# Row statistics by one VectorE instruction, and another order of score products, in a two-layer attention tower

## The reference

```
h = token_table[x] * (x != 0) + position_table[...]       # a scan over steps gives the positions
h = h + attention0(layernorm(h))                          # softmax(q k^T / 8) times the normalised rows
h = h + routed_ffn(layernorm(h))                          # relu, two layers of 128, an expert chosen per group of rows
h = h + attention1(layernorm(h))                          # with biases, values and an output projection
h = h + mixture_ffn(layernorm(h))                         # top 2 of 8 gates, gelu, two products for each expert

layernorm(x) = (x - mean(x)) / sqrt(var(x) + 1e-5)        # over the 64 features of a row
```

## Time and profile before

| | |
|---|---|
| runs shown | 999.9, 999.84, 1001.16 us; median 999.9 us |
| profiled execution | 1000.58 us, span of the core 998.8 us |
| TensorE matmuls busy | 933.3 us (93%) |
| VectorE busy | 663.6 us (66%) |
| ScalarE busy | 541.9 us (54%) |
| GpSimd busy | 489.4 us (49%) |
| mean granted clock of TensorE | 0.993 of full speed |
| chain that ended last | TensorE 75%, VectorE 11%, GpSimd 7%, issue 5% |

### The profile page before, as it was taken

One profiled execution on the slowest core, in us unless ns is written; L12 is line 12 of the kernel. 1 busy time (PEld: TensorE's weight loads), 2 busy tenths in 40 slices (PEclk: granted clock), 3 DMA queues, 4 the chain that ended last, 5 costly groups with the idle time before them and its releaser, 6 DMA issues.

```text
span 998.8 us, 21041 instructions
## 1 busy us (share of the span) xinstructions
PE 933.3 (93%) x6247; PEld 635.2 (64%) x6262; DVE 663.6 (66%) x1839; ACT 541.9 (54%) x1067; POOL 489.4 (49%) x779
## 2 busy tenths in 40 slices
PE   4879999999998888889999999998999999999998
PEld 3656666666665555555666666666766667767665
DVE  5868788888887888877888878886434344344331
ACT  1335555555555555544555555555566556655664
POOL 0064545545457888883455554544343433434410
PEclk9989999999999999998999999999999999999999
DMA  3000000000001222210000000000000000000000
GB/s 97 3 1 1 1 0 0 0 0 0 1 1 49 58 63 54 64 33 1 1 1 0 0 0 0 1 1 2 11 17 11 16 16 11 16 15 11 16 11 22
DMA packets 18991, 15.10 MB, mean 15 GB/s; under 512 B 5762, under 2 KB 18946, under 8 KB 18946
## 3 DMA queue, kind: packets, MB, share of 16 engines
q1 hardware_dynamic: 18946, 14.52, 5.2%
HBM read 10.32 MB, written 4.19 MB: 15 GB/s over the span
## 4 chain that ended last, share of the span: by engine, by line
PE 75%; DVE 11%; POOL 7%; issue 5%; DMA 1%; DVEq 0%; ACT 0%; POOLq 0%; SPq 0%
PE bank L1205 12%; PE bank L1027 7%; PE bank L1036 7%; PE bank L1185 7%; PE bank L1028 6%; DVE nmax L723 6%; PE bank L1186 6%; PE bank L1002 6%; PE bank L949 5%; PE bank L1015 4%; PE bank L974 3%; POOL stat L353 2%; PE bank L991 2%; PE bank L1195 2%; PE bank L992 2%
## 5 line engine op out<-in xcount | busy, mean ns | idle before, releaser
L360 POOL TENSOR_TENSOR XN<-XC,stat 128x252 f32<-128x252 f32 x128 | 85.3, 666 | 216.0 <-PE bank L1036 210.9
L723 DVE TENSOR_REDUCE nmax<-bank 128x1 fp32r<-128x512 f32 x256 | 165.0, 686 | 34.6 <-PE bank L1002 29.9
L353 POOL TENSOR_TENSOR stat<-stat,half 128x4 f32<-128x4 f32 x128 | 134.1, 1048 | 91.1 <-DVE stat L641 88.3
L496 ACT ACTIVATE PT<-bank 128x512 f32<-128x512 f32 x256 | 139.5, 595 | 45.9 <-PE bank L1028 45.3
L1036 PE MATMUL bank<-PT,XN 128*64 128x256 f32 x1024 | 138.3, 392 | 0.0
L545 ACT ACTIVATE PT<-bank 128x512 f32<-128x512 f32 x256 | 132.0, 605 | 11.2 <-PE bank L1186 11.1
L468 ACT ACTIVATE OT<-bank 128x256 f32<-128x256 f32 x96 | 36.8, 384 | 183.1 <-PE bank L1036 132.2
L1205 PE MATMUL bank<-PT,W 128*64 128x256 f32 x1024 | 122.8, 382 | 0.0
L446 ACT ACTIVATE X<-bank 128x512 fp32r<-128x512 f32 x128 | 76.3, 596 | 78.7 <-PE bank L949 78.7
L1027 PE MATMUL bank<-QH,X 128*128 128x512 f32 x256 | 116.0, 453 | 0.5 <-ACT Q L489 0.4
L1185 PE MATMUL bank<-X,WH 128*128 128x512 f32 x256 | 107.5, 420 | 0.8 <-ACT K L536 0.8
(11 more groups left out here) (135 smaller groups left out, 1679.7 us busy)
## 6 DMA issues: line engine op xcount, KB each, us to landing
WR<-experts SPq DMA_DIRECT2D x64, 129.0 KB, 2.0
out<-H SPq DMA_DIRECT2D x32, 128.0 KB, 1.7
W<-pack SPq DMA_DIRECT2D x5, 252.5 KB, 4.0
W<-pack SPq DMA_DIRECT2D x1, 251.0 KB, 5.1
W<-pack SPq DMA_DIRECT2D x1, 243.0 KB, 5.7
tk<-tokens SPq DMA_DIRECT2D x1, 64.0 KB, 4.4
route_sb<-route SPq DMA_DIRECT2D x1, 0.2 KB
```

The costliest lines, as they stand in the source:

```text
L353: pl.tensor_tensor(stat[:, par, 3, :], stat[:, par, 2, :], half[:, :], ALU.pow).then_inc(sigma_done, 1)
L496: sc_.activation(PT[:, par, kt, :], bank[4 + kt % 2][:, :], ACT.Exp, scale=SCALE).then_inc(s.e_ready, 1)
L723: v.tensor_reduce(nmax[:, par, t:t + 1], bank[2 + t % 2][:, :], axis=AX, op=ALU.max, negate=True).then_inc(s.max_ready, 1)
```

## The change

The mean and the variance of a row are taken by VectorE's mean-and-variance instruction straight from `H`: one `bn_stats` for each of the four row tiles (64 elements each, six numbers out), and one `bn_aggr` for each, which makes mean and variance of the six. A memset puts epsilon into a small tile and one addition adds the variance to it. The sum, the squares, their sum and the scaling on VectorE go, and so does GpSimd's multiplication by -1/64. GpSimd does one piece of work for each sequence (`norm`): power, subtraction of the mean, and the scaling as before. `XC` has one buffer in place of two.

In the bodies the two halves of VectorE's part have new places. `moments` (the four `bn_stats`) stands, for sequence i+4, in attention after `finish` and ahead of the last two maxima, in the routed stage and in the mixture where the sum was. `moments_end` (the rest) stands after the last maximum, and where the squares were.

In attention, the first two maxima stand ahead of `finish`. On TensorE the products for maxima stand one each after the second and the third score tile and two after the fourth, and the values of all four tiles follow in one row.

The core of the diff (declarations of tiles and semaphores, and the arguments of the calls, are left out):

```diff
-            def norm_centre(s, before, phase, i, par):
-                pool.wait_ge(s.sum_ready, i + 1)
-                pl.tensor_tensor(stat[:, par, 1, :], stat[:, par, 0, :], ninv[:, :], ALU.mult).then_inc(mean_done, 1)
...
-                pl.tensor_tensor(XC[:, par, :, :], hb(i), over(stat[:, par, 1, :], D), ALU.add)\
-                    .then_inc(s.xc_ready, 1)
-
-            def norm_scale(s, before, phase, i, par, lane):
+            def norm(s, before, phase, i, par, lane):
 
                 pool.wait_ge(s.var_ready, i + 1)
-                pl.tensor_tensor(stat[:, par, 3, :], stat[:, par, 2, :], half[:, :], ALU.pow).then_inc(sigma_done, 1)
+                pl.tensor_tensor(rstd[:, :], VE[:, par, :], half[:, :], ALU.pow).then_inc(sigma_done, 1)
+                pl.tensor_tensor(XC[:, :, 1:D], H[:, bass.ds(i, 1), :, 1:D].rearrange("p a t d -> p (a t) d"),
+                                 over(MV[:, par, :, 0], D - 1), ALU.subtract).then_inc(s.xc_ready, 1)
                 pool.wait_ge(sigma_done, phase * NSEQ + i + 1)
+                pool.wait_ge(s.xc_ready, i + 1)
...
-            def norm_sum(s, i, par):
-                v.tensor_reduce(stat[:, par, 0, :], hb(i), axis=AX, op=ALU.add).then_inc(s.sum_ready, 1)
-
-            def norm_squares(s, i, par):
...
+            def moments(s, i, par):
+
+                for t in range(NT):
+                    ins = v.bn_stats(ST[:, par, t, :], H[:, bass.ds(i, 1), t, :].rearrange("p a d -> p (a d)"))
+                ins.then_inc(s.stats_ready, 1)
+
+            def moments_end(s, before, i, par):
+                dve.wait_ge(s.stats_ready, i + 1)
+                if not known(i) or i >= 2:
+                    dve.wait_ge(s.xc_ready, i - 1)
+                elif before is not None:
+                    dve.wait_ge(before.xc_ready, NSEQ - 1 + i)
+                v.memset(VE[:, par, :], EPS)
+                for t in range(NT):
+                    ins = v.bn_aggr(MV[:, par, t, :], ST[:, par, t, :])
+                ins.then_inc(s.pair_ready, 1)
+                dve.wait_ge(s.pair_ready, i + 1)
+                v.tensor_tensor(VE[:, par, :], VE[:, par, :], MV[:, par, :, 1], ALU.add).then_inc(s.var_ready, 1)
 
             def first_norms(s, i):
 
-                par = i % 2
                 dve.wait_ge(h0_ready, i + 1)
-                norm_sum(s, i, par)
-                if i >= 1:
-                    norm_squares(s, i - 1, 1 - par)
-                if i == 3:
-                    norm_sum(s, 4, 0)
-                    norm_squares(s, 3, 1)
+                moments(s, i, i % 2)
+                moments_end(s, None, i, i % 2)
...
                 def body(i, par):
-                    squares_on(s, after, i + 4, par)
-                    sum_on(s, after, i + 5, 1 - par)
                     if has(i + 1):
                         low_parts(i + 1, 1 - par)
+                        maxima(i + 1, 1 - par, range(2))
                     if not known(i) or i >= 1:
                         finish(i - 1, 1 - par)
+                    moments_on(s, after, i + 4, par)
                     if has(i + 1):
-                        maxima(i + 1, 1 - par)
+                        maxima(i + 1, 1 - par, range(2, NT))
+                    moments_end_on(s, before, after, i + 4, par)
...
                     scores(i, par, 1)
+                    if has(i + 1):
+                        scores_for_max(i + 1, 1 - par, 0)
                     if not known(i) or i >= 1:
                         turn_back(s, before, i - 1, 1 - par)
                     scores(i, par, 2)
+                    if has(i + 1):
+                        scores_for_max(i + 1, 1 - par, 1)
                     scores(i, par, 3)
                     if has(i + 1):
-                        scores_for_max(i + 1, 1 - par, 0)
-                        scores_for_max(i + 1, 1 - par, 1)
+                        scores_for_max(i + 1, 1 - par, 2)
+                        scores_for_max(i + 1, 1 - par, 3)
...
-                    values(i, par, lane, 0)
-                    values(i, par, lane, 1)
-                    if has(i + 1):
-                        scores_for_max(i + 1, 1 - par, 2)
-                        scores_for_max(i + 1, 1 - par, 3)
-                    values(i, par, lane, 2)
-                    values(i, par, lane, 3)
+                    for kt in range(NT):
+                        values(i, par, lane, kt)
```

More of the change, by code:

```diff
@@ L40 @@
 CENTRE, LOWER, FUSE, FUSED, NORM = 8, 15, 17, 20, 24
-CONSTS = 7
+CONSTS = 6
 HIGHS, LOWS = 5, 4
@@ L77, in __init__ @@
         self.xh_done = sem(f"{tag}_xh_done")
-        self.sqsum_ready = sem(f"{tag}_sqsum_ready")
-        self.sum_ready = sem(f"{tag}_sum_ready")
+        self.stats_ready = sem(f"{tag}_stats_ready")
+        self.pair_ready = sem(f"{tag}_pair_ready")
         self.xc_ready = sem(f"{tag}_xc_ready")
-        self.sq_ready = sem(f"{tag}_sq_ready")
         self.var_ready = sem(f"{tag}_var_ready")
@@ L210, in tower_kernel @@
         half = sb("half", [P, NT])
-        ninv = sb("ninv", [P, NT])
+        rstd = sb("rstd", [P, NT])
         route_sb = sb("route_sb", [1, NSEQ * NG], I32)
@@ L226, in tower_kernel @@
         OP = sb("OP", [P, 2, SEQ], BF16)
[L228 to L231, removed]
+        ST = sb("ST", [P, 2, NT, 6])
+        VE = sb("VE", [P, 2, NT])
+        MV = sb("MV", [P, 2, NT, 2])
+        XC = sb("XC", [P, NT, D])
         XN = sb("XN", [P, 4, NT, D])
@@ L277, in tower_kernel @@
         dve_chain, gate_chain = sem("dve_chain"), sem("gate_chain")
-        mean_done, sigma_done, xn_done = sem("mean_done"), sem("sigma_done"), sem("xn_done")
+        sigma_done, xn_done = sem("sigma_done"), sem("xn_done")
         consts_set, ids_ready, pos_ready, parts_ready, prod_ready, fused_ready, prod_read = (
@@ L328, in _ @@
             pl.memset(half[:, :], -0.5).then_inc(consts_set, 1)
-            pl.memset(ninv[:, :], -1.0 / D).then_inc(consts_set, 1)
             pl.memset(MK[:, :, :], 0.0).then_inc(consts_set, 1)
@@ L358, in norm_scale @@
                     pool.wait_ge(before.o_ps, NSEQ - 3 + i)
-                scale = over(stat[:, par, 3, :], D - 1)
-                pl.tensor_tensor(XN[:, lane, :, 1:D], XC[:, par, :, 1:D], scale, ALU.mult).then_inc(xn_done, 1)
+                scale = over(rstd[:, :], D - 1)
+                pl.tensor_tensor(XN[:, lane, :, 1:D], XC[:, :, 1:D], scale, ALU.mult).then_inc(xn_done, 1)
                 if not known(i) or i >= 2:
@@ L369, in norm_scale, with norm_on @@
                                  ALU.subtract).then_inc(s.xs_ready, 1)
-            def centre_on(s, before, after, phase, i, par):
+            def norm_on(s, before, after, phase, i, par, lane):
                 if has(i):
-                    norm_centre(s, before, phase, i, par)
+                    norm(s, before, phase, i, par, lane)
                 elif after is not None:
[L376 to L382, removed]
+                    norm(after, s, phase + 1, i - NSEQ, par, lane)
             def norms(s, before, after, phase):
                 def body(i, par, lane):
-                    centre_on(s, before, after, phase, i + 4, par)
-                    scale_on(s, before, after, phase, i + 3, 1 - par, (lane + 3) % 4)
+                    norm_on(s, before, after, phase, i + 3, 1 - par, (lane + 3) % 4)
                 sweep4(pool, body)
-            norm_centre(a0, None, 0, 0, 0)
             for i in range(3):
-                norm_centre(a0, None, 0, i + 1, 1 - i % 2)
-                norm_scale(a0, None, 0, i, i % 2, i)
+                norm(a0, None, 0, i, i % 2, i)
             norms(a0, None, f0, 0)
@@ L697, in _, with moments_on, moments_end_on, attention @@
                     first_norms(a0, (i - NORM) // 2)
-            def sum_on(s, after, i, par):
+            def moments_on(s, after, i, par):
                 if has(i):
-                    norm_sum(s, i, par)
+                    moments(s, i, par)
                 elif after is not None:
                     dve.wait_ge(s.h_done, i - NSEQ + 1)
-                    norm_sum(after, i - NSEQ, par)
-            def squares_on(s, after, i, par):
+                    moments(after, i - NSEQ, par)
+            def moments_end_on(s, before, after, i, par):
                 if has(i):
-                    norm_squares(s, i, par)
+                    moments_end(s, before, i, par)
                 elif after is not None:
-                    norm_squares(after, i - NSEQ, par)
-            def attention(s, after, base, meanwhile):
+                    moments_end(after, s, i - NSEQ, par)
+            def attention(s, before, after, base, meanwhile):
                 def low_parts(i, par):
@@ L718, in low_parts, with maxima @@
                                     ALU.subtract).then_inc(s.ql_ready, 1)
-                def maxima(i, par):
-                    for t in range(NT):
+                def maxima(i, par, tiles):
+                    for t in tiles:
```

(21 more changed lines are left out.)

14 lines of the change are left out of this document (1 added, 13 removed).

## The result

The changed kernel takes 1002.38 us (median of 12 runs, 1001.45 to 1005.3) against 1000.72 for the kernel before (12 runs, 999.84 to 1001.27): ratio 1.0023, 95% interval 1.0014 to 1.0033. It is slower by about 1.7 us; 10 were forecast (1010 against 999.9). The profiled execution took 1004.23 (span 1002.4), one of the longer ones.

What follows compares the result with a forecast made beforehand. VectorE was taken to end each attention sequence, a two-sequence chain to pace the routed stage, TensorE to fill the mixture. From 1000.58: +18 - 1 - 4 - 3 = +10, 1010.6, given as 1010 us; range 992 to 1030.

Steps and rivals of the forecast that it cites:

- the attention term, "+18": Attention: statistics ahead of the last two maxima delay each sequence's end by 0.30 us, over 60 sequences +18.
- B: Attention, VectorE: time of the four statistics instructions ahead of maximum 2, taken as about 0.6 us from MAX8 rows.
- the 0.42: Attention: worked-out delay of maximum 2, starting at +6.43 us after the spreading instead of +6.01.
- the deduction of 0.12: Attention: delay cut from 0.42 to 0.30 for covered exponential waits and 10 of 32 sequences without address arithmetic.
- The 0.28: Attention, TensorE: time assumed for product 0, from two products in a row taking 0.55 us.
- Start: Before attention: no wait for GpSimd's centring, one sum dropped, squares moved; -3 us, between -1.4 and -4.05.
- Routed stage: Routed feed-forward: chain over two sequences falls from 8.95 to 8.65 us, 0.15 per sequence over 28 sequences, -4.
- Mixture: TensorE is full there; statistics replace a sum of 0.42 us within the gate's chain, hidden, at no cost.
- Rival 1: Attention: the order wins if maximum 2 starts no later than before; 992 us, or 977 at TensorE's limit; chance 0.2.
- Rival 2: Statistics at 0.2 to 0.25 us each, 0.8 to 1.0 for four, giving 1025 to 1040 us; chance 0.2.
- The argument from the loop counter: Statistics read H at loop-counter addresses, adding sequencer time: an addition on H starts 0.14 us after its product, against 0.04.
- Rival 3: Routed stage: no gain, since centring now stands behind the power; 1014 us, within the forecast's range, no separate chance.

Runs made afterwards that it cites:

- experiment 5: The changed kernel itself, unedited, run again on one chip beside the kernel before: 1002.98 us.
- experiments 1 and 3: First: changed kernel with attention statistics behind maxima 2 and 3, 971.89 us. Second: new product and maxima order with the old statistics, 980.33 us.
- the parts alone: Against the kernel before: new order with old statistics, 980.33 us; new statistics behind the last maximum, with all maxima still behind the division, 989.9 us.
- experiment 4: The changed kernel with the four attention statistics instructions issued twice, the first four into a buffer nobody reads: 1031.89 us, ratio 1.0317.

## Why the prediction was off

The sign and the mechanism held: VectorE without a wait for another engine from maximum 1 to maximum 3, TensorE waiting for a maximum in each sequence, the low parts behind over 1 us of idle time. The size did not: +10 was forecast, +1.7 came.

- **The step that failed is the attention term, "+18".** It is the small difference of two long sums of offsets, and the parts came from rows that held a wait, from the mean of an unequal pair, and, for B, from another instruction. Offset by offset from the spreading's start: product 0 at +2.39 as forecast; its own time 0.23 (202.50 to 202.73) and not 0.28; the turning back 0.36 and not 0.46; the score tile 0.54 and not 0.53; so product 1 at +3.52 and not +3.66. Maximum 1 to statistics takes 1.73 (1.74 forecast). B, the four statistics, is 0.51 and not 0.6. Maximum 2 therefore starts at +6.18, 0.17 later than before where 0.42 was worked out and 0.30 taken. Of the 0.25 by which the 0.42 was too much, 0.14 lies ahead of product 1 and 0.09 in B; the deduction of 0.12 covered half of it. The 0.28 was the mean of two distances, 0.23 from product to product and 0.32 from the second product to the values. Over the 60 distances behind the first of each stage the sequence grew by 0.19 on average, +11.2, and the two first ones gave back 0.8 (0.3 in experiment 5). Together the attention costs 4.61 + 5.75 = +10.4, not +17. The turning back's 0.46 held a wait: in the kernel before, the third score tile starts at 205.11, 0.05 after the end of the exponential whose bank it needs, and in the change some 0.2 after it. That exponential in the kernel before:
```profile
204.46 0.60 ACT L496 ACTIVATE PT<-bank 128x512 f32<-128x512 f32 x1 [0.38 <-PE bank L1028]
```
- **Start:** -4.55 for -3. TensorE's idle time ahead of an embedding fell from 4.05 to 0.67 at its longest near the end, where "near 1" was expected.
- **Routed stage:** -4.61 for -4, by the forecast's own steps: turning to statistics 2.56 (2.58), statistics and second layer 1.30 (1.47), aggregation to power 0.78 (0.75), power to turning 3.95 (3.85); together 8.59 (8.65).
- **Mixture:** its sequences kept 9.53, at no cost, as forecast. The 0.64 at its entry was not foreseen: the body's last statistics stand ahead of the first gate chain.
- **Together:** -4.55 + 10.4 - 4.6 + 0.6 - 0.3 = +1.6.
- **Rival 1** was the kernel one move away. Its point, maximum 2 not later than +6.01, was missed by 0.17; with the statistics behind it the limit that it names, TensorE's own row of about 7.1, is what experiments 1 and 3 run at (7.06 to 7.11). The prediction weighed the two parts as one bundle and did not say that the parts alone are worth -19 and -10.
- **Rival 2** (statistics 0.2 to 0.25 each) is out. The four starts are 0.13 apart: 0.51 in all in the change and 0.50 to 0.52 in experiment 4, below the 0.156 each that was worked out from the MAX8 rows and half of the 0.25 from the RECIPROCAL. The argument from the loop counter did not carry over: the addition on H starts 0.14 to 0.15 after its product in the loop's sequences and 0.03 in those written out, but the four statistics take 0.51 to 0.52 to the first start behind them in both. The Trainium skill's rule, VectorE: DVE Perf Modes (The TRN2 errata), by which small SBUF-source instructions each pay a fixed cost of about 150 cycles, gives an estimated 0.22 for one and 0.89 for the four. The length of one row, 0.21, agrees with it; the distance between two that follow each other without a wait, 0.13, does not, since their rows overlap. The measurement decides.
- **Rival 3** (no gain in the routed stage) is out: the stage took 4.61 less.

## What to carry to other kernels

Read a duration from a start-to-start distance only where nothing waits between the two starts; a stage that is to be reordered can hold distances that contain waits, and the reorder takes them away. When a change puts work ahead of the instruction that ends a step, look for the idle time on the same engine behind that instruction: here 1.40 us stood free, and moving four instructions by two places turned a loss of 2 to 3 us into a gain of 28 to 30. And when two edits come together, price each alone as well as both: one of them may be hiding the other's gain.

## Not expected of the hardware

- Four mean-and-variance instructions of 64 elements take 0.50 to 0.52 us from the first start to the next instruction's, though each is 0.21 long (0.60 from the first start to the last end, starts 0.13 apart); four aggregations with the memset take 0.41 (207.49 to 207.90).
- Stretches of TensorE at the half clock differ between executions of one kernel: the mixture's first interval took 8.24 in one and 6.30 in the other, after equal TensorE work (5.17 busy of 6.90 in both). A difference of about 2 us between two profiled executions can't by itself be put down to an edit.
